# Attention and routed experts on one core: a new order for the routing, the expert rows and the base stores

## What is computed

```
x = x + attention(layernorm(x), ctx, ctx, lens)
xt = layernorm(x).reshape(1024, 256)
probs = softmax(xt @ Wg); eidx = argmax(probs); gate = probs[eidx]
pos = (cumsum(one_hot(eidx)) * one_hot(eidx)).sum(-1) - 1      # place in the expert
flat = eidx * 128 + pos  if pos < 128  else dropped
xd = zeros(8 * 128, 256); xd[flat] = xt
oe = (silu(xd @ W1) * (xd @ W3)) @ W2                           # each expert its own weights
shared = (silu(xt @ sw1) * (xt @ sw3)) @ sw2
x = x + gate * oe[flat] + shared                                # no expert term if dropped
```

## Time and profile before

| | |
|---|---|
| median of 3 runs | 159.66 us (159.27 to 159.71) |
| the profiled execution | 160.15 us, span 158.3 us |
| TensorE matmul busy | 147.8 us, 93% of the span |
| VectorE, ScalarE, GpSimd busy | 99.3, 81.6, 67.6 us |
| DMA | 18.42 MB, mean 116 GB/s |

### The profile page before, as it was taken

The page is one execution under the profiler, slowest core; times in us unless marked ns, Lnnn a source line. Parts: engine busy times, 40 slices in busy tenths (PEclk is TensorE's granted clock), DMA queues, the critical chain, the costliest instruction groups (busy, mean ns, idle before and its releaser), DMA issues.

```text
span 158.3 us, 3414 instructions
## 1 busy us (share of the span) xinstructions
PE 147.8 (93%) x1256; PEld 99.2 (63%) x1256; DVE 99.3 (63%) x232; ACT 81.6 (52%) x179; POOL 67.6 (43%) x100
## 2 busy tenths in 40 slices
PE   7999999989999999999999999999798999999940
PEld 2465555455556555554554778678695987999720
DVE  0599886688786878875222547877572368776220
ACT  3544364755747485746676267644301585663300
POOL 7124949106409050503969300065700068728650
PEclk9999999999999999999999999999999999999998
DMA  3992716271342600000430099512438402221210
GB/s 79 346 354 75 233 42 206 77 242 39 115 160 68 206 2 4 0 6 0 148 134 2 2 326 315 183 48 86 162 119 237 139 33 83 67 66 64 96 60 33
DMA packets 15824, 18.42 MB, mean 116 GB/s; under 512 B 1980, under 2 KB 15077, under 8 KB 15808
## 3 DMA queue, kind: packets, MB, share of 16 engines
q1 hardware_dynamic: 14368, 14.98, 29.8%
q0 software_dynamic: 1152, 2.97, 5.7%
q10 hardware_dynamic: 288, 0.26, 0.5%
HBM read 14.12 MB, written 4.21 MB: 116 GB/s over the span
## 4 chain that ended last, share of the span: by engine, by line
PE 77%; DMA 8%; DVE 6%; issue 2%; ACT 1%; POOL 1%; SPq 1%; POOLq 0%; DVEq 0%
PE bank L995 18%; PE bank L1032 11%; PE bank L1016 9%; PE bank L1243 5%; PE bank L1096 5%; PE bank L1097 5%; PE bank L1184 4%; DMA out<-xs 4%; PE bank L947 3%; PE bank L1046 3%; PE bank L1218 2%; PE bank L1219 2%; DMA xs<-in_x 2%; DMA xs<-out,rk 2%; PE bank L1058 2%
## 5 line engine op out<-in xcount | busy, mean ns | idle before, releaser
L536 DVE TENSOR_REDUCE nm<-bank 128x2 f32<-128x512 f32 x64 | 40.8, 684 | 10.3 <-PE bank L995 10.3
L789 ACT ACTIVATE pt<-bank 128x512 f32<-128x512 f32 x64 | 34.5, 589 | 15.8 <-PE bank L1016 15.6
L1016 PE MATMUL bank<-qz,kz 32*128 32x256 f32 x256 | 40.8, 402 | 0.0
L995 PE MATMUL bank<-kz,qz 32*128 32x256 f32 x256 | 35.1, 403 | 0.2 <-DVE qz L513 0.2
L995 PEld LDWEIGHTS bank<-kz,qz 32*128 32x128 f32 x256 | 21.9, 184 | 13.0 <-issue 7.2
L1016 PEld LDWEIGHTS bank<-qz,kz 32*128 32x128 f32 x256 | 24.9, 184 | 4.5 <-ACT pt L789 2.8
L1032 PE MATMUL bank<-pt,vext 128*32 128x256 f32 x256 | 20.2, 391 | 0.0
L381 POOL TENSOR_SCALAR qz<-xs,rs,mrs 128x256 f32<-128x256 f32 x14 | 7.7, 562 | 20.0 <-DVE mrs L507 20.0
L460 POOL DMA_INDIRECT expert_rows<-rk,idx_s x8 | 8.3, 1037 | 18.4 <-DVE rk L626 16.5
L475 POOL DMA_INDIRECT xs<-out,rk x8 | 9.7, 1212 | 14.5 <-DMA out<-xs 12.3
L947 PE MATMUL bank<-onesb 128*128 128x512 bf16 x34 | 11.4, 477 | 1.0 <-POOL onesb L375 1.0
(11 more groups left out here) (155 smaller groups left out, 304.4 us busy)
## 6 DMA issues: line engine op xcount, KB each, us to landing
wraw<-in_w SPq DMA_DIRECT2D x10, 352.0 KB, 3.4
wlate<-in_w SPq DMA_DIRECT2D x6, 352.0 KB, 4.6
wraw<-in_w SPq DMA_DIRECT2D x10, 128.0 KB, 3.4
expert_rows<-zero SPq DMA_DIRECT2D x1, 1032.0 KB, 6.2
out<-xs SPq DMA_DIRECT2D x8, 128.0 KB, 3.4
xs<-in_x SPq DMA_DIRECT2D x3, 256.0 KB, 4.9
cs<-in_ctx SPq DMA_DIRECT2D x3, 256.0 KB, 5.4
wlate<-in_w SPq DMA_DIRECT2D x6, 128.0 KB, 4.3
```

Source lines behind the costliest of these rows:

```text
L536: nc.vector.tensor_reduce(nm[:, b % 2, :, place], scores_bank[:].rearrange("p (u c) -> p u c", u=2), AX_X, ALU.max, negate=True).then_inc( ...
L789: nc.scalar.activation(pt[:, g % NPT, n % 4, :], sc_bank[n % NS][:], ACT.Exp).then_inc(exped, 1)
L995: mm = nc.tensor.matmul(scores_bank[:, u * D:(u + 1) * D], qz[rows, b, half, u * P:(u + 1) * P], kz[rows, b, half, :], start=True, stop=True)
L1016: mm = nc.tensor.matmul(sc_bank[n % NS][:, c * D:(c + 1) * D], kz[rows, b, half, c * P:(c + 1) * P], qz[rows, b, half, :], start=True, sto ...
```

## The change

- The second half's piece with the logits, (1, 2), becomes piece 2 of `UPS`, (0, 1) piece 3. Which banks a piece uses is now in a table, `UP_BANK`; piece 2 takes the first bank pair again and piece 3 the third, and TensorE's waits for a free bank follow the table. The half pieces come in the order (3,0), (2,0), count of the first half, (2,1), (3,1), second logits, (4,0), count of the second half, (4,1), (5,0), (5,1).
- `ROUTE` has gates ahead of row numbers, `weigh_tokens` runs before `find_rows`, and the sends wait for `idx` instead of `gate`.
- VectorE's and ScalarE's lists are put in another order; the first base addition goes before the last low part, and the last base addition behind the low part of expert 0's rows.
- SyncE's loads of the expert rows and the last four base stores come by turns.
- TensorE turns expert 0's rows ahead of the last down-projection, and two wide matmuls whose output nobody reads are gone.

```diff
@@ -114,11 +114,12 @@
 
 
 
-ROUTE = ("lmax", "ldif", "cand", "first", "oh", "cum", "pos", "past", "slot", "idx", "rec", "lsum", "ltwo",
-         "gate")
+ROUTE = ("lmax", "ldif", "cand", "first", "oh", "rec", "lsum", "ltwo", "gate", "cum", "pos", "past", "slot",
+         "idx")
 ROUTED = ((0, 4), (4, B))
 HALF = B // 2
-UPS = ((0, 2), (0, 0), (0, 1), (1, 2), (1, 0), (1, 1))
+UPS = ((0, 2), (0, 0), (1, 2), (0, 1), (1, 0), (1, 1))
+UP_BANK = (0, 1, 0, 2, 1, 2)
 ROWS_OF = (P, P, FL)
 
 
@@ -358,14 +359,24 @@
                 sp.wait_ge(shared_added, b + 1)
                 sp.dma_start(out[b], xs[:, b, :]).then_inc(base_stored, 16)
 
+            def load_rows(i):
+
+                a, z = LOADS[i]
+                if i == 0:
+                    sp.wait_ge(xd_sent, 16 * B)
+                xd = xd_dram.rearrange("(n p) d -> p n d", p=P)
+                sp.dma_start(xe[:, a:z, :], xd[:, a:z, :]).then_inc(ld_xe[i], 16)
+
             for b in range(HALF):
                 store_base(b)
-            sp.wait_ge(xd_sent, 16 * B)
-            xd = xd_dram.rearrange("(n p) d -> p n d", p=P)
-            for i, (a, z) in enumerate(LOADS):
-                sp.dma_start(xe[:, a:z, :], xd[:, a:z, :]).then_inc(ld_xe[i], 16)
-            for b in range(HALF, B):
-                store_base(b)
+            load_rows(0)
+            load_rows(1)
+            store_base(4)
+            store_base(5)
+            load_rows(2)
+            store_base(6)
+            store_base(7)
+            load_rows(3)
 
         @block.gpsimd
         def _(pool):
@@ -455,7 +466,7 @@
                 pool.wait_ge(xd_zeroed, 16)
                 pool.wait_ge(x2_made, z)
                 pool.wait_ge(numbered, 1)
-                pool.wait_ge(route, routed(part, "gate"))
+                pool.wait_ge(route, routed(part, "idx"))
                 for b in range(a, z):
                     nc.gpsimd.indirect_dma_start(
                         xd_dram, bass.IndirectOffsetOnAxis(ap=idx_s[:, b:b + 1], axis=0), x2[:, b, :], None,
@@ -629,7 +640,7 @@
 
                 rows = ROWS_OF[UPS[k][1]]
                 dve.wait_ge(silu_done, k + 1)
-                nc.vector.tensor_tensor(sig[k % 3][0:rows], u3_bank[k % 3][0:rows, :], sig[k % 3][0:rows],
+                nc.vector.tensor_tensor(sig[k % 3][0:rows], u3_bank[UP_BANK[k]][0:rows, :], sig[k % 3][0:rows],
                                         ALU.mult).then_inc(h_made, 1)
 
             for t in range(TAIL):
@@ -706,30 +717,32 @@
             dve.wait_ge(shifted, NH)
             nc.vector.memset(he[:, :, F:], 0.0).then_inc(hpad_set, 1)
             token_norm(B - 1)
-            choose(0)
             low_tokens(B - 1)
             shared_hidden(0)
+            choose(0)
             shared_hidden(1)
+            weigh_tokens(0)
+            find_rows(0)
             shared_low(0)
+            shared_low(1)
             shared_hidden(2)
-            shared_low(1)
-            find_rows(0)
-            weigh_tokens(0)
+            choose(1)
+            shared_hidden(3)
+            weigh_tokens(1)
+            find_rows(1)
             shared_low(2)
-            shared_hidden(3)
-            choose(1)
             shared_low(3)
             shared_hidden(4)
-            find_rows(1)
-            weigh_tokens(1)
             shared_low(4)
             shared_hidden(5)
+            shared_add(0)
             shared_low(5)
-            for b in range(B):
+            for b in range(1, B - 1):
                 shared_add(b)
                 if b in (3, 5):
                     expert_low(2, (b - 3) // 2)
             rows_low(0)
+            shared_add(B - 1)
             rows_low(1)
             for e in range(E):
                 expert_hidden(e)
@@ -819,7 +832,7 @@
                 act.wait_ge(up_done, k + 1)
                 if k >= 3:
                     act.wait_ge(h_lo, k - 2)
-                nc.scalar.activation(sig[k % 3][0:rows], u1_bank[k % 3][0:rows, :], ACT.Silu).then_inc(silu_done, 1)
+                nc.scalar.activation(sig[k % 3][0:rows], u1_bank[UP_BANK[k]][0:rows, :], ACT.Silu).then_inc(silu_done, 1)
 
             def shared_logits(half):
 
@@ -899,15 +912,15 @@
             high_tokens(B - 1)
             shared_silu(0)
             shared_silu(1)
+            shared_high(0)
             half_tanh(0)
-            shared_high(0)
             shared_high(1)
+            shared_logits(1)
             shared_silu(2)
+            shared_silu(3)
             shared_high(2)
-            shared_logits(1)
-            shared_silu(3)
+            half_tanh(1)
             shared_high(3)
-            half_tanh(1)
             shared_silu(4)
             shared_high(4)
             shared_silu(5)
@@ -1082,12 +1095,12 @@
                         pe.wait_ge(s_lo, len(SHARED_PIECES))
                     if k == 1:
                         pe.wait_ge(exped, NH)
-                    if k >= 3:
-                        pe.wait_ge(h_made, k - 2)
-                    if k == 3:
+                    if k == 2:
                         pe.wait_ge(lg_copied, 1)
+                    if UP_BANK[k] in UP_BANK[:k]:
+                        pe.wait_ge(h_made, max(i for i in range(k) if UP_BANK[i] == UP_BANK[k]) + 1)
                 n1, n3 = ROWS_OF[f] + (WG if f == 2 else 0), ROWS_OF[f]
-                u1, u3 = (of[k % 3][0:n, :].rearrange("p (b t) -> p b t", b=HALF)
+                u1, u3 = (of[UP_BANK[k]][0:n, :].rearrange("p (b t) -> p b t", b=HALF)
                           for of, n in ((u1_bank, n1), (u3_bank, n3)))
                 for xpart, parts in ((xhi, (shi, slo)), (xlo, (shi,))):
                     tokens = xpart[:, HALF * half:HALF * (half + 1), c, :]
@@ -1170,8 +1183,8 @@
 
                 half, j = divmod(b, HALF)
                 if b == 0:
-                    pe.wait_ge(h_lo, 3)
-                    pe.wait_ge(h_made, 4)
+                    pe.wait_ge(h_lo, UPS.index((0, 1)) + 1)
+                    pe.wait_ge(h_made, UPS.index((1, 2)) + 1)
                     pe.wait_ge(lg_copied, 2)
                 if b == HALF:
                     pe.wait_ge(h_lo, len(UPS))
@@ -1191,7 +1204,7 @@
                 pe.wait_ge(ld_xe[next(i for i, (a, z) in enumerate(LOADS) if a <= e < z)], 16)
                 if e == 0:
                     pe.wait_ge(h_made, len(UPS))
-                    pe.wait_ge(route, routed(len(ROUTED) - 1, "gate"))
+                    pe.wait_ge(route, routed(len(ROUTED) - 1, "idx"))
                 if e >= 5:
                     pe.wait_ge(e_out, e - 4)
                 rows_bank = ht_bank[e] if e < 2 else y_bank[e % 2]
@@ -1250,24 +1263,21 @@
             shared_up(1, 1)
             turn_tokens(B - 1)
             turn_logits(0)
+            shared_up(3, 0)
             shared_up(2, 0)
+            count_tokens(0)
             shared_up(2, 1)
-            shared_up(3, 0)
-            count_tokens(0)
             shared_up(3, 1)
+            turn_logits(1)
             shared_up(4, 0)
-            turn_logits(1)
+            count_tokens(1)
             shared_up(4, 1)
             shared_up(5, 0)
-            count_tokens(1)
             shared_up(5, 1)
-            for b in range(B):
+            for b in range(B - 1):
                 shared_down(b)
-            pe.wait_ge(route, routed(len(ROUTED) - 1, "cum"))
-            for _ in range(2):
-                nc.tensor.matmul(counts[:].rearrange("p (n c) -> p n c", c=P), onesb[:],
-                                 onesb[:].unsqueeze(1).broadcast_to([P, 4, P]), start=True, stop=True)
             turn_rows(0)
+            shared_down(B - 1)
             turn_rows(1)
             for e in range(E):
                 expert_up(e)
```

## The result

The changed kernel takes 157.14 us in the median of 4 executions (156.94 to 157.20), the kernel before 159.47 us (159.22 to 159.71) beside it: a ratio of 0.9856 with a 95% interval of 0.9835 to 0.9877, so 2.3 us or 1.4% faster. That is inside the range given, and less than the 3.1 us forecast. The ratios here and in the table of experiments leave out executions over 1.5% above the fastest of the same kernel (three in experiment 11, one in experiment 12); medians and counts are of all. The profiled execution took 157.20 us, 2.95 less than the profiled one of before. The two figures differ, 2.3 between medians and 2.95 between profiles, and the first two experiments are about that.

A forecast was written before the change was run, and what follows sets the result against it. TensorE's own sequence and waits bound the kernel, at most 3.7 us removable. Gains of 2.75 (first expert) - 0.15 (third load) + 0.5 (gathers) = 3.1 us, from the 159.66 median to 156.6; range 155.9 to 158.3.

The forecast's parts named there:

- The order of the up pieces: TensorE's up-projection: same work reordered, second logits one half piece earlier at 101.66, no stall; cost taken as 0.
- Step 3: Base addition 1 ahead of the last subtraction: no hole before the third down-projection, fourth and later about 1.25 us earlier.
- the forecast's own 156.0 to 157.1: Range of the main case, from the 3.7 us ceiling to a late third load and thin covers; chance 0.62.
- Step 4: Loads and stores by turns, wide matmuls gone: first row load at 114.15, first expert at 118.0, 2.75 us gained.
- The 0.15 us for the third load: Allowance for SyncE's third row load, issued after store 6, landing after its rows are wanted at 120.0.
- Step 5: Gathers: store 8 issued 2 us earlier, taken to land in 4 us, so expert 1's down-projection gains 0.5 us.
- B: Rival, rows come late: sends, landing or SyncE's turn take 0.5 to 1.5 us more; 157.1 to 158.1; chance 0.17.
- C: Rival: store 8 lands as late as before, gather holds the output addition; 157.4 middle, 158.2 worst; chance 0.11.
- E: Rival: TensorE's clock falls to 1.2 GHz at the first experts, up to 2.03 us each, kernel slower; chance 0.04.
- the rule on the interfaces shared by GpSimd and VectorE: Skill rule: VectorE instructions with two SBUF inputs contend with GpSimd; the gain would fall by what sends lengthen, no figure.

The follow-up runs named there:

- experiment 11: Changed kernel with row numbers ahead of gates and the sends waiting for the gates; median 159.38 us (157.38 to 161.77), ratio 0.9981 to the kernel before.
- experiment 12: Changed kernel with the second logits' transposes inside half piece (3,1), meant half a microsecond earlier; median 157.64 us, ratio 0.9884 to the kernel before.
- experiment 1: The kernel before, unchanged, run and profiled once more; median 159.20 us, ratio 0.9996.
- experiment 2: Kernel before with only the tail changed (stores and loads by turns, base addition 1 and row turns earlier, wide matmuls gone); median 160.65 us, ratio 1.0069.
- experiment 4: Changed kernel with the first row load ahead of base store 4 in SyncE's queue; median 156.74 us, ratio 0.9864 to the kernel before.
- experiment 3: Changed kernel with its tail put back to that of before, so routing alone; median 159.00 us, ratio 0.9987 to the kernel before.
- experiment 5: The changed kernel, unchanged, run again on a second chip; median 157.11 us, ratio 0.9864 to the kernel before.
- experiment 7: Changed kernel with all four row loads ahead of the last four base stores, as before; median 157.05 us, ratio 0.9863 to the kernel before.
- experiment 9: Changed kernel with base addition 1 behind the last low part again; median 158.51 us, ratio 0.9942 to the kernel before.
- experiment 10: Changed kernel with the two wide matmuls put back ahead of expert 0's row transposes; median 157.08 us, ratio 0.9855 to the kernel before.
- experiment 6: Changed kernel with the first row load ahead of base store 4, run again beside the changed kernel; median 157.38 us, ratio 0.9864 to the kernel before.
- experiment 8: Kernel before with only the tail changed but the two wide matmuls kept; median 160.76 us, ratio 1.0081 to the kernel before.

## Why the prediction was right, and where its sizes were off

**Steps that held.** The order of the up pieces cost nothing, and the second logits, both halves' row numbers, the first and last send, the third down-projection without a hole and the fourth at its date all came within 0.15 us of the working. Step 3's size is confirmed by taking its addition back: 1.1 us at the transposes. So is the idea that the rows' date and TensorE's own date must move together: each half of the change alone gave 0.17 us or nothing. The measured 157.14 lies at the upper edge of the forecast's own 156.0 to 157.1, not at its 156.6; the mechanism was right, and the gain in the sum was too large by what follows.

**Step 4, the first row load at 114.15.** It came at 114.61. I had both bounds, the sends and store 4, and gave the load to the sends; experiment 4 shows that the sends would have let it go by 114.19, and that SyncE's queue adds about 0.8 us from the issue of store 4 (113.84) to the load behind it. The same 0.76 to 0.77 us lie between them in experiments 3, 5, 7, 9, 10 and 12. The working had store 4 at 113.75 and the load 0.4 later. That is 0.4 us of the 2.75 for the first expert. The 0.15 us for the third load was not paid in the changed kernel; it is the next bound, as experiment 6 shows.

**Step 5, 0.5 us at expert 1.** The mechanism is right in the profile shown, and gone in the profile after. But it was in that execution alone: in experiment 1 nothing on TensorE waited for the gather. With the 0.3 us of the rows' date in the same execution, 0.8 us of the sum was made against a profile 0.5 us over its median, and I subtracted it from the median all the same. The sum as it should have stood: 3.1 - 0.5 - 0.3 - 0.45 + 0.15 = 2.0 us, and the later comparisons give 2.1 (159.21 to 157.11).

**Credit given to the wrong part.** The turns of stores and loads (experiment 7) and the removal of the wide matmuls (experiment 10) are each worth nothing. The gathers moved by 5.5 us; in experiment 1 VectorE had waited 0.57 us for the first of them, and TensorE not at all.

**Rivals.** B, the rows late, is what happened in small: 0.5 us, by SyncE's turn. C did not occur: store 8 landed in 2.1 us. E did not occur in the changed kernel: its granted clock is full until TensorE has ended. Experiments 2 and 8 have two groups that go with the mean granted clock, so its mechanism is a likely price of this stretch, about 1.5 us, with a hole of 2.0 to 2.4 us; it was not seen in a profile.

**The sends beside VectorE.** The prediction read from two sums, 5.04 and 5.08 us, that VectorE's work doesn't slow the sends. The single sends show that it does:

```profile
106.11 1.28 DVE L677 TENSOR_TENSOR hTlo<-late,hThi 96x512 fp32r<-96x512 f32 x2
...
110.93 0.69 DVE L677 TENSOR_TENSOR hTlo<-late,hThi 128x512 fp32r<-128x512 f32 x1 [0.35 <-ACT hThi L852]
```

These subtractions of the changed kernel have both operands in SBUF. The send at 107.05 starts with 0.34 us of the pair in the first row left and takes 1.19 us; the one at 111.10 starts with 0.52 us of the second row left and takes 1.38. In experiment 12, with 0.25 us left, it takes 1.10. Over the fourteen profiles 26 sends start in this way, and each takes 0.97 us and what is left of the subtraction, less 0.11 to 0.13. The others take 0.97 to 0.99, beside a product that reads PSUM too (110.02), but for the first send of each execution, 1.20 to 1.28. So the trace agrees with the rule on the interfaces shared by GpSimd and VectorE (the Trainium skill, GPSIMD Engine Reference, section 8). It is read from durations; no run changed this alone. The second half's four sends took 112.48 - 107.05 = 5.43 us against 5.08: 0.22 and 0.41 us were added to two of them, where before it was 0.29 to one (1.26 us at 111.30). The changed kernel lost nothing by it, since SyncE held the load longer; in experiment 4, whose load waits for the sends, it may.

## What to carry to other kernels

Where two paths end in one instruction, price both ends before giving a gain to either: here the routing alone was worth 0.17 us, the tail alone nothing, the two together 2.1. Before a wait in a profile is put into a sum, hold the profiled execution's time against the median; if it is above, a second profile tells which waits belong to the kernel. Here a load that stood behind a store in one queue went out at the queue's pace behind it though what it waits for was done. A sum over several instructions can hide that one of them is slowed: look at the single durations and at what ran beside them.

## What the runs showed that I had not expected

- A row load behind a base store on SyncE goes out 0.77 us after the store's issue (113.84 to 114.61); ahead of it, it went out at 114.19, and the store then 0.77 us later (114.96).
- Two groups of executions 1.4 to 1.5 us apart where TensorE waits over 2 us for rows, with mean granted clocks of 0.992 to 0.996 and 0.976 to 0.986 (20 executions); and at the end of the program a fall to half of full speed 2.1 to 5.1 us after the last recorded matmul.
- A 128 KB base store landed in 2.1 us in the median in the changed kernel and in 3.4 in the one before, where 1032 KB of row loads went out just ahead of the last four (2.9 in experiment 7, which has this order too).
- An indirect send on GpSimd that starts while VectorE subtracts with both operands in SBUF takes 1.10 to 1.40 us instead of 0.97, the longer the more of the subtraction is left (26 sends in fourteen profiles).
- The order of gates and row numbers, with the same instructions, went with executions from 157.38 to 161.77 us; the cause is open.
